# Edge attention in a graph network: the weighted sums of the values, in another number format and array shape

## What is computed

```python
qkv = x @ W_qkv.T + b_qkv
Q, K, V = jnp.split(qkv, [DK * HEADS, 2 * DK * HEADS], axis=-1)
...
scores = jnp.einsum('ehd,ehd->eh', Q[receivers], K[senders]) * scale
smax = jax.ops.segment_max(scores, receivers, num_segments=n_nodes)
ex = jnp.exp(scores - smax[receivers])
denom = jax.ops.segment_sum(ex, receivers, num_segments=n_nodes)
att = ex / denom[receivers]
out = jax.ops.segment_sum(att[:, :, None] * V[senders], receivers, num_segments=n_nodes)
```

## Time and profile before

| | |
|---|---|
| time before, median of 3 runs | 2308.41 us |
| lowest and highest run | 2305.57, 2312.28 us |
| the profiled execution: its own time | 2311.25 us |
| its span, first to last instruction | 2309.5 us |
| mean granted clock of TensorE, of full speed | 0.934 |
| TensorE busy (matmuls) | 1985.3 us, 86% |
| VectorE busy | 1403.4 us, 61% |
| ScalarE busy | 797.6 us, 35% |
| 1301 sums: 800 matmul records, 112.4 us | mean 287 ns |
| 1290 transposes: 800 records, 118.6 us | mean 280 ns |
| 1279 scores: 480 records, 115.1 us | mean 376 ns |
| 1346 minimum: 80, 116.8 us | mean 1460 ns |

### The profile page before, as it was taken

The page is one execution under the profiler, slowest core; times in us unless marked ns, Lnnn a source line. Parts: engine busy times, 40 slices in busy tenths (PEclk is TensorE's granted clock), DMA queues, the critical chain, the costliest instruction groups (busy, mean ns, idle before and its releaser), DMA issues. The chain is left out here.

```text
span 2309.5 us, 31827 instructions
## 1 busy us (share of the span) xinstructions
PE 1985.3 (86%) x10098; PEld 1147.6 (50%) x10099; DVE 1403.4 (61%) x3988; ACT 797.6 (35%) x1911; POOL 771.7 (33%) x849
## 2 busy tenths in 40 slices
PE   7987879889889888877769897699999884999997
PEld 4344343333333333333234453388888644777775
DVE  5885078988988988988753154288778643111111
ACT  2024134334343333343221230177777520222221
POOL 0000057777777777777700000011111000122221
PEclk9998989989989989989889898899999995999999
DMA  4012179999999999999930081535423143333351
GB/s 152 6 52 114 59 293 394 407 407 397 408 408 398 396 406 399 401 394 398 399 138 0 24 271 63 162 119 141 142 84 101 35 162 117 105 109 107 109 183 27
DMA packets 144378, 490.09 MB, mean 212 GB/s; under 512 B 16766, under 2 KB 17438, under 8 KB 144000
## 3 DMA queue, kind: packets, MB, share of 16 engines
q0 software_dynamic: 99952, 353.16, 40.5%
q1 hardware_dynamic: 44304, 135.43, 17.4%
HBM read 449.86 MB, written 38.67 MB: 212 GB/s over the span
## 5 line engine op out<-in xcount | busy, mean ns | idle before, releaser
L545 POOL DMA_INDIRECT m_ring<-in_table,m_rows_at x640 | 651.0, 1017 | 235.4 <-issue 130.8
L816 PE MATMUL m_acc<-m_ring,m_diag 64*64 64x512 f32 x2560 | 466.1, 699 | 131.7 <-ACT m_diag L716 131.1
L605 DVE CUSTOM_DVE_ANT_0 m_ring<-m_ring,m_coming,m_part 128x512 f32<-128x512 f32 x640 | 443.6, 749 | 47.6 <-DMA m_ring<-in_table,m_rows_at 37.2
L816 PEld LDWEIGHTS m_acc<-m_ring,m_diag 64*64 64x64 f32 x2560 | 152.1, 149 | 414.4 <-ACT m_diag L716 341.7
L716 ACT ACTIVATE m_diag<-m_eye,m_inner 128x64 f32<-128x64 f32 x640 | 222.3, 348 | 308.2 <-DVE m_inner L605 308.2
L1864 PEld LDWEIGHTS e_psU<-e_rowsT,x_w 128*128 128x128 f32 x1472 | 170.2, 194 | 14.1 <-issue 14.1
L1864 PE MATMUL e_psU<-e_rowsT,x_w 128*128 128x128 f32 x1472 | 170.7, 278 | 2.8 <-DMA x_w<-in_we 1.7
L1356 DVE TENSOR_TENSOR a_pT<-a_psT,a_pT 128x512 fp32r<-128x512 f32 (+1 forms) x240 | 140.1, 599 | 40.3 <-ACT a_pT L1391 37.0
L1873 PE MATMUL e_psY<-x_w,e_hT 128*128 128x512 f32 x368 | 161.7, 592 | 0.0
L1391 ACT ACTIVATE a_pT<-a_psT 128x512 fp32r<-128x512 f32 (+1 forms) x240 | 122.6, 528 | 97.5 <-PE a_psT L1290 97.5
L1290 PE MATMUL a_psT<-ident,a_prob 128*128 128x128 f32 x800 | 118.6, 280 | 28.4 <-ACT a_prob L1385 20.0
(11 more groups left out here) (326 smaller groups left out, 2705.6 us busy)
## 6 DMA issues: line engine op xcount, KB each, us to landing
x_w<-in_we SPq DMA_DIRECT2D x16, 2048.0 KB, 10.6
xnT<-edge_log_counts SPq DMA_DIRECT2D x40, 640.0 KB, 3.9
m_ring<-in_table,m_rows_at POOLq DMA_INDIRECT x640, 7.8
qk_parts<-p_parts SPq DMA_DIRECT2D x32, 320.0 KB, 4.2
a_k<-qk_parts SPq DMA_DIRECT2D x32, 320.0 KB, 9.2
edge_shares<-shareT SPq DMA_DIRECT2D x10, 640.0 KB, 3.0
m_share<-edge_shares SPq DMA_DIRECT2D x10, 640.0 KB, 7.4
edge_log_counts<-p_log_cnt SPq DMA_DIRECT2D x10, 640.0 KB, 6.2
```

The lines of the kernel that those rows point to most:

```text
L545: pool.indirect_dma_start(ring[:, slot, :], None, ins["table"], bass.IndirectOffsetOnAxis(rows_at[:, h, k:k + 1], 0)).then_inc(s_land[slot ...
L605: dve.tensor_tensor_reduce(ring[:, slot, 0:D], ring[:, slot, 0:D], coming[:, t % 2, :], part[:, b, k:k + 1], 0.0, ALU.mult, ALU.add, inner ...
L816: mm = pe.matmul(acc[to, i, :], diag[rows, h % 2 * TOPK + k, :], ring[rows, nth % RING, D:2 * D], start=h == 0 and k < 2, stop=h == HEADS ...
```

## The change

Probabilities and values are no longer split. `v` is float32, [P, NT, D]: VectorE adds the bias straight into it. The turned probabilities are copied once, in float32: piece 0 by ScalarE, pieces 1 and 2 by VectorE. The sums are made for four units at once (two node tiles of two heads): for each of ten sender tiles one float32 matmul for each head, stationary the 64 columns of that head, moving the 256 columns of its two node tiles; head 0 writes the partitions 0 to 63 of `psU`, head 1 64 to 127, so that each stands in one half of TensorE's columns. The result of four units is one [128, 256] tile, which two float32 transposes turn (`turn_back`); four `message` instructions follow. The matrix `fold` goes. The sums' pieces keep their places in TensorE's order, but for every fourth unit instead of every second.

```diff
@@ stage_projections
-        v_row = sb("v_row", [P, 2, D])
...
-                dve.tensor_tensor(v_row[:, t % 2, :], psV[:, t % 2, :], bv[:, :], ALU.add).then_inc(s["vout"], 1)
-                dve.drain()
-                rows = v_row[:, t % 2, :].rearrange("p (h d) -> p h d", h=HEADS)
-                dve.tensor_copy(v[:, t, :, 0, :], rows)
-                dve.drain()
-                dve.tensor_tensor(v[:, t, :, 1, :], rows, v[:, t, :, 0, :], ALU.subtract)
+                dve.tensor_tensor(v[:, t, :], psV[:, t % 2, :], bv[:, :], ALU.add).then_inc(s["vout"], 1)
@@ stage_edge_attention
-        prob, pT = sb("prob", [P, 2, NP]), sb("pT", [P, 2, NT, 2, P], F32R)
+        prob, pT = sb("prob", [P, 2, NP]), sb("pT", [P, NT, 2, 2, P])
...
                 if n:
-                    pe.wait_ge(s["rest"], 3 * n - 2 + piece)
+                    pe.wait_ge(s[f"copied{piece}"], n)
...
             def sums(g, piece):
-                m, t, h = unit(2 * g)
+                m = unit(4 * g)[0]
                 a, z = THIRDS[piece]
-                pe.wait_ge(s["rest"], 6 * g + 4 + piece)
+                pe.wait_ge(s[f"copied{piece}"], 4 * g + 4)
                 if piece == 0 and g:
                     pe.wait_ge(s["both"], g)
                 for x in range(a, z):
-                    for part in range(2):
-                        mm = pe.matmul(psU[:, 0:2 * P], v[:, x, 2 * m + h, :, :].rearrange("p a d -> p (a d)"),
-                                       pT[:, part, x, :, :].rearrange("p t n -> p (t n)"),
-                                       start=x + part == 0, stop=x + part == NT)
+                    for h in range(2):
+                        mm = pe.matmul(psU[64 * h:64 * h + 64, 0:2 * P], v[:, x, (2 * m + h) * 64:(2 * m + h + 1) * 64],
+                                       pT[:, x, h, :, :].rearrange("p t n -> p (t n)"), start=x == 0, stop=x == NT - 1)
...
-            def add_halves(g):
+            def turn_back(g):
                 pe.wait_ge(s["both"], g + 1)
                 if g:
-                    pe.wait_ge(s["msg"], 2 * g)
+                    pe.wait_ge(s["msg"], 4 * g)
                 for b in range(2):
-                    mm = pe.matmul(psM[:, 64 * b:64 * b + 64], both[:, b, :], fold[:, :], start=True, stop=True)
-                mm.then_inc(s["folded"], 1)
+                    mm = pe.transpose(psM[:, b * P:(b + 1) * P], both[:, b, :], c.ident[:, :])
+                mm.then_inc(s["back"], 1)
...
             for n in range(UNITS):
-                g = n // 2
-                if n % 2 == 0 and g:
+                g = n // 4
+                if n % 4 == 0 and g:
                     sums(g - 1, 1)
                 turn(n, 0)
-                if n % 2 == 0 and g:
+                if n % 4 == 0 and g:
                     sums(g - 1, 2)
                 turn(n, 1)
                 turn(n, 2)
                 if n + 2 < UNITS:
                     score(n + 2)
-                if n % 2:
+                if n % 4 == 3:
                     sums(g, 0)
-                elif g:
-                    add_halves(g - 1)
+                elif n % 4 == 0 and g:
+                    turn_back(g - 1)
@@ VectorE
-            def rest(n, piece):
+            def keep_turned(n, piece):
                 a, z = THIRDS[piece]
-                dve.wait_ge(s["high"], 3 * n + piece + 1)
-                dve.tensor_tensor(pT[:, 1, a:z, n % 2, :], psT[:, piece, 0:(z - a) * P].rearrange("p (a n) -> p a n", n=P),
-                                  pT[:, 0, a:z, n % 2, :], ALU.subtract).then_inc(s["rest"], 1)
+                m, tile, h = unit(n)
+                dve.wait_ge(s["turned"], 3 * n + piece + 1)
+                dve.tensor_copy(pT[:, a:z, h, tile % 2, :], psT[:, piece, 0:(z - a) * P].rearrange("p (a n) -> p a n", n=P))\
+                    .then_inc(s[f"copied{piece}"], 1)
...
             for n in range(UNITS):
-                rest(n, 0)
-                rest(n, 1)
+                keep_turned(n, 1)
+                keep_turned(n, 2)
                 if n + 2 < UNITS:
                     lowest(n + 2)
-                rest(n, 2)
-                if n % 2:
-                    shares(n // 2)
+                if n % 4 == 3:
+                    shares(n // 4)
@@ ScalarE
             for n in range(UNITS):
-                g = n // 2
-                high(n, 0)
-                high(n, 1)
-                if n % 2 == 0 and g:
+                g = n // 4
+                keep_turned(n)
+                if n % 4 == 0 and g:
                     keep_sums(g - 1)
                 if n + 1 < UNITS:
                     exponent(n + 1)
-                if n % 2 and g:
+                if n % 4 == 1 and g:
                     message(g - 1)
-                high(n, 2)
```

More of the change, by code:

```diff
@@ L1221, in stage_edge_attention @@
         q, k = sb("q", [P, 4, P], F32R), sb("k", [P, 2, 2, 2, NP], F32R)
-        prob, pT = sb("prob", [P, 2, NP]), sb("pT", [P, 2, NT, 2, P], F32R)
-        low, den, rden = sb("low", [P, 2]), sb("den", [P, 4]), sb("rden", [P, 4])
-        both, fold = sb("both", [P, 2, P]), sb("fold", [P, 64])
+        prob, pT = sb("prob", [P, 2, NP]), sb("pT", [P, NT, 2, 2, P])
+        low, den, rden = sb("low", [P, 2]), sb("den", [P, 8]), sb("rden", [P, 8])
+        both = sb("both", [P, 2, P])
         psS, psT, psU, psM = ps("psS", [P, 3 * D]), ps("psT", [P, 3, D]), ps("psU", [P, D]), ps("psM", [P, D])
-        names = ("score", "low", "exp", "turned", "high", "rest", "sums", "both", "folded", "msg", "rden", "pad", "fold", "ahead",
+        names = ("score", "low", "exp", "turned", "copied0", "copied1", "copied2", "sums", "both", "back", "msg", "rden", "pad", "ahead",
                  "q0", "q1", "q2", "q3", "k0", "k1", "log0", "log1", "log2", "log3")
@@ L1385, in exponent, with keep_turned @@
                 act.activation(prob[:, n % 2, 0:N], prob[:, n % 2, 0:N], ACT.Exp, bias=low[:, n % 2:n % 2 + 1], scale=-1.0,
-                               accum_out=den[:, n % 4:n % 4 + 1]).then_inc(s["exp"], 1)
-            def high(n, piece):
-                a, z = THIRDS[piece]
-                act.wait_ge(s["turned"], 3 * n + piece + 1)
-                act.activation(pT[:, 0, a:z, n % 2, :], psT[:, piece, 0:(z - a) * P].rearrange("p (a n) -> p a n", n=P),
-                               ACT.Copy).then_inc(s["high"], 1)
+                               accum_out=den[:, n % 8:n % 8 + 1]).then_inc(s["exp"], 1)
+            def keep_turned(n):
+                a, z = THIRDS[0]
+                m, tile, h = unit(n)
+                act.wait_ge(s["turned"], 3 * n + 1)
+                act.activation(pT[:, a:z, h, tile % 2, :], psT[:, 0, 0:(z - a) * P].rearrange("p (a n) -> p a n", n=P),
+                               ACT.Copy).then_inc(s["copied0"], 1)
             def keep_sums(g):
@@ L1396, in keep_sums @@
                 if g:
-                    act.wait_ge(s["folded"], g)
+                    act.wait_ge(s["back"], g)
                 act.activation(both[:, :, :], psU[:, 0:2 * P].rearrange("p (b n) -> p b n", b=2), ACT.Copy).then_inc(s["both"], 1)
             def message(g):
-                act.wait_ge(s["folded"], g + 1)
+                act.wait_ge(s["back"], g + 1)
                 act.wait_ge(s["rden"], g + 1)
-                for b in range(2):
-                    m, t, h = unit(2 * g + b)
-                    i = g % 2 * 2 + b
-                    act.activation(msg[:, m * NT + t, 64 * h:64 * h + 64], psM[:, 64 * b:64 * b + 64], ACT.Copy,
-                                   scale=rden[:, i:i + 1]).then_inc(s["msg"], 1)
+                for i in range(4):
+                    m, tile, h = unit(4 * g + i)
+                    at = g % 2 * 4 + i
+                    act.activation(msg[:, m * NT + tile, 64 * h:64 * h + 64], psM[:, i % 2 * P + 64 * h:i % 2 * P + 64 * h + 64],
+                                   ACT.Copy, scale=rden[:, at:at + 1]).then_inc(s["msg"], 1)
             exponent(0)
             for n in range(UNITS):
-                g = n // 2
-                high(n, 0)
-                high(n, 1)
-                if n % 2 == 0 and g:
+                g = n // 4
+                keep_turned(n)
+                if n % 4 == 0 and g:
                     keep_sums(g - 1)
@@ L1417, in _ @@
                     exponent(n + 1)
[L1418 removed]
+                if n % 4 == 1 and g:
                     message(g - 1)
[L1420 to L1422 removed]
+            keep_sums(UNITS // 4 - 1)
+            message(UNITS // 4 - 1)
 def stage_join(c, msg, weights, ahead):
```

22 lines of the change are left out of this document (9 added, 13 removed).

## The result

The changed kernel takes 2311.50 us, the median of 20 runs (2306.37 to 2318.07). The kernel before, beside it on the same chip, takes 2306.01 us (20 runs, 2300.79 to 2312.28). The ratio is 1.0019 with a 95% interval of 1.0010 to 1.0027. So the change costs about 4.4 us where 5.4 us of gain were forecast (4.4 is also the difference of the two means; the medians lie 5.5 apart). The time lies in the predicted range and within the 0.3% that was called no change, but the sign of the central forecast is wrong: the interval excludes any gain.

A forecast was written before the change was run, and what follows sets the result against it. TensorE was taken as nearly full before; afterwards score-minimum rounds plus lumped sums bound it. Exponentials 6.83 us less, the end 1.48 more: net gain 5.4 us, from 2308.41 to 2303.0 us; range 2295 to 2324.

The forecast's parts named there:

- the wake: Edge attention, from the minimum's end to the waiting score's start: 0.08 us, taken between 0.05 and 0.15, in 60 rounds.
- the change of shape: TensorE switching array shape between sums and scores or transposes: 0.09 us each, four a group, 0.36 us.
- the stage's end: Edge attention from the last exponential to the end: 9.38 us instead of 7.90, 1.48 more.
- The sums: TensorE's float32 sums for four units: column halves run together, 0.216 us a pair of passes, 4.32 us a group.
- The first rival: Weight loads of the sums not hidden: 0.10 us for each of 200 pairs, 20 us, 2323; chance 0.10.
- the second: Rival: the sums' column halves run one after the other, 4.3 us more in each of 20 groups, 2389; chance 0.05.
- The chain: Edge attention: one long step and three rounds of score and minimum (3.24 or 3.35 us), 16.87 us a group against 17.1.
- full drain: TensorE emptied at each change of shape: 0.16 us instead of 0.09, 5.6 us more over 80 changes, forecast 2309.
- The third rival: TensorE's clock falls in a group's 10 us without sums: 21 us for one round a group, 2324, all three 64; chance 0.05.
- the ends that the prediction named for them: Uncertainty in the edge attention: 60 wakes give -1.8 to +4.2 us, 80 changes of shape -7.2 to +5.6.
- TensorE's share in the stage: Sign in the edge attention: if TensorE's busy share stays at nine tenths, the forecast of score waits and rounds is wrong.
- a full TensorE: Rival: TensorE stays full and waits go, 14.3 us a group, 2252; said to be forbidden by one score buffer; chance 0.07.

The follow-up runs named there:

- the same-half kernel: The changed kernel with both heads' sums in the same column half, so their passes can't run side by side: 2393.79 us in one run.
- the first experiment: The changed kernel with the waits for queries, keys and new counts passed earlier, so score and minimum each wait for one thing: 2305.22 us, ratio 0.9988.
- second experiment: The changed kernel with all three thirds of a group's sums side by side, two changes of array shape a group instead of four: 2305.34 us, ratio 0.9988.
- the kernel in four places: The changed kernel with two buffers for turned probabilities, sums spread behind all four scores of the next group, and waits moved ahead: 2265.54 us, ratio 0.9805.

## Why the prediction was wrong

Two terms of its chain were too small, the wake, taken 60 times, and the change of shape, taken 80 times; together they used up the gain. That it became a loss comes mostly from the stage's end, where the forecast had put nothing for TensorE's lower clock. Point by point, by its own steps.

*The sums: right.* The passes start in pairs, and the pairs follow each other by 0.216 us. The first two, the first six and the first eight passes of a group, TensorE after the change, each from a narrower stretch:

```profile
1656.91 0.44 PE L1295 MATMUL a_psU<-a_pT,v 128*64 128x256 f32 x2
...
1656.91 0.87 PE L1295 MATMUL a_psU<-a_pT,v 128*64 128x256 f32 x6
...
1656.91 1.08 PE L1295 MATMUL a_psU<-a_pT,v 128*64 128x256 f32 x8
```

Two passes end 0.44 us after the first starts, two more cost 0.21 or 0.22. The first rival, loads that are not hidden, is out, and the same-half kernel shows what the second would have cost. The form that no row of before had, 128 rows by 64 columns, behaves as the quarters of the earlier trace rows suggested. The Trainium skill's page TensorE: Matmul & The Clock Gate, Part 3, The mechanism, lets a weight load pass a running matmul for another row group or into the background buffer. Here the row groups are the same and the loads (0.137 us each) cost the pairs nothing, so of the two only the second case can apply.

*The chain: right.* One long step and three rounds in each group, three waits for the minimum, VectorE's and ScalarE's relief off the path, nothing from the V products. The long part came out at 7.16 us where 7.04 were summed, the three rounds at 9.97 where 9.83 were: 0.26 us a group too little in all. Over 18 groups that makes 4.7 us; first to last exponential is 337.14 us where 331.83 were forecast, 5.3 more.

*The first failed step: the wake, 0.08 us.* It was taken between 0.05 and 0.15 and "nearer to the row at full clock". But the row of 0.05 is a sum that waits for one thing, and the only row in which this very score waited for the minimum said 0.15. I put that down to the half clock; the first experiment shows that it is the second wait. At full clock it is 0.15 too, and 0.06 without the second wait. Against this the round's other parts came out a little shorter (from the score's start to the minimum's 1.43 or 1.54 for 1.45 and 1.56), so that a round is 0.04 to 0.06 longer than forecast and not 0.07.

*The second failed step: the change of shape, 0.09 us.* What the 0.09 stood for came true: from the score's last pass (256 columns, fp32r) to the first sum is 0.21 us, where such a pass otherwise takes 0.12.

```profile
1656.70 0.28 PE L1273 MATMUL a_psS<-a_k,a_q 128*128 128x256 f32 x1
```

What it left out is that the first pass behind a change starts with its weight load and lasts 0.05 us longer: 0.430 instead of 0.379 for a sum, and four transposes behind a change take 0.66 where they took 0.60. So a change costs 0.14 to 0.15. In the timeline above, 32 passes take 3.60 us to the next transpose (16 pairs are 3.46, so 0.14), four transposes 0.59 to the next sum (0.44, so 0.15), eight passes 1.01 (0.86, so 0.15), six transposes 0.63 to the score (0.58 in the earlier trace rows, so 0.05), and from the score to the sums it is 1.33 for 1.26. Together 0.56 us a group against 0.36. Against this the transposes were priced too high, six at 0.66 where the earlier trace rows has 0.58 up to the score, so that the forecast's long part is 0.12 us too short and not 0.20. The rows had a hint of the 0.05: a pass that starts with its load lasts 0.64 us and one whose load came early 0.59. The prediction used that pair of durations for a rival and not for this term. The Trainium skill's page TensorEngine Tiling (Array Packing), Key Properties, has a change of tiling mode drain TensorE. The forecast named 0.16 us a change as its own price for a full drain and 2309 us as the result; with about 0.145 for a change, that reading was the nearer one.

*The third failed step: the stage's end, and the clock in it.* The tail was to take 9.38 us from the last exponential and took 10.78 (1823.51 to 1833.36 + 0.93). The rows of after:

```profile
1823.51 1.34 ACT L1376 ACTIVATE a_prob<-a_prob,a_low 128x1250 f32<-128x1250 f32 x1 [0.50 <-DVE a_low L1342]
...
1824.99 2.03 PE L1284 MATMUL a_psT<-ident,a_prob 128*128 128x128 f32 x10 [1.96 <-ACT a_prob L1376]
...
1826.95 5.45 PE L1295 MATMUL a_psU<-a_pT,v 128*64 128x256 f32 x40
...
1833.36 0.93 ACT L1398 ACTIVATE msg<-a_psM,a_rden 128x64 f32<-128x64 f32 x4 [0.53 <-PE a_psM L1305]
```

Ten transposes last 2.03 us instead of 1.31 and the sums 5.45 instead of 4.54 (second experiment). The clock is why; two stretches in this place:

```profile
1822.00:1825.40 3.40, 1.44 (x14) 1.20 (x13) 2.33 (x5) 2.44 (x6) 0.00 (x0) 1.00 0.00 0
1825.40:1828.80 3.40, 3.40 (x19) 2.31 (x19) 1.27 (x4) 0.60 (x1) 0.00 (x0) 0.50 0.00 0
```

TensorE was busy for 1.44 of 3.40 us and was then granted 0.50 for the next stretch, its lower level of 1.2 GHz. This is the third rival, in a place where I had not looked for it: in the rounds, at 1.00 from 1500 to 1780 us, it did not come true. The terms of the sum were sound: in the first two experiments, at full clock, the tail takes 9.25 us. But there the lower clock comes a little later, at the start of the join. The kernel of the first experiment, then the kernel before:

```profile
1818.81:1822.22 3.41, 1.09 (x9) 0.55 (x6) 0.32 (x1) 1.31 (x5) 0.00 (x0) 1.00 0.00 0
1822.22:1825.63 3.41, 3.41 (x10) 2.13 (x9) 0.37 (x1) 2.48 (x3) 0.00 (x0) 0.50 0.61 160
```

```profile
1832.20:1835.60 3.40, 2.16 (x11) 1.48 (x12) 0.69 (x1) 1.85 (x4) 0.00 (x0) 1.00 0.25 63
1835.60:1839.00 3.40, 3.40 (x13) 1.68 (x12) 0.69 (x1) 0.64 (x1) 0.00 (x0) 1.00 0.37 102
```

Of the ten traces, the kernel before and the one that only moves its waits have no such stretch between the last exponential and the end of the join. The other eight all have one, in the tail (both heads in one column half) or at the start of the join; the changed kernel alone has both, the second at 1835.70 to 1839.10. The join takes 56.8 us in the three traces without a low stretch in it, and 57.8 to 58.3 in the seven with one. So the 1.3 us there come with the longer tail, hardly by chance; the 1.4 us in the changed kernel's own tail are seen in the one trace that there is of it.

The account: between the 5.4 us less that were forecast and the 3.9 more of the profiled execution lie 9.3. Of these, 5.3 are between the first and the last exponential, from the rounds and changes of shape; 1.4 are in the tail and 1.3 in the join; 0.35 lie ahead of the first exponential, which comes 4.78 us after the first score instead of 4.43 (VectorE stands 0.44 us before its masking instruction, for no reason that the profile shows). The 0.9 that remain lie in other stages, and traces differ by that much where the code is the same: from the end of the join to the end they take 418.4 to 421.2 us. The line of the forecast was close to its own figure (0.40 each for faster and no change). Two terms of hundredths of a microsecond, taken 60 and 80 times, took the gain away; the clock and the rest made it a loss. Both errors lay inside the ends that the prediction named for them (+4.2 and +5.6), and for both I took a value below the one that was measured. The two ends together are 2312.8 us; the 2309 at which the prediction let its own case stop was less than their sum.

*A sign that was badly chosen.* "If TensorE's share in the stage stays at nine tenths, the chain is wrong": it is 248.64 of 280, 0.89 (0.92 before), and the chain is right. A pass of a pair is followed by the next pair after 0.216 us and is shown as lasting 0.379, so busy time closes over part of the gap at the end of each run of matmuls. The idle time before the scores, 33.3 us in 300, was the sign to name.

*What the prediction did not ask.* It costed the arrangement as given and stated that the transposes fit inside a round. The next question, what else would fit there, leads to the kernel in four places. That one score buffer forbids a full TensorE holds for this arrangement alone: the four-places kernel has TensorE full with the one buffer, at 14.78 us a group. The rounds are a bound only while they have less than 3.2 us of TensorE's work in them; spread evenly, every unit has 3.7.

## What to carry to other kernels

When an engine's work is cut, look at whether the rest still stands where that engine is the bound: with a latency loop between two engines (here score and minimum, 3.23 us), work moved into the loop's idle time costs little (a group fell from 17.17 to 15.42 us, though two changes of shape were added), and the same work in one lump is paid in full. Keep an instruction at the end of such a loop waiting for one thing; pass its other waits earlier, where time is idle. Price a term that occurs 60 or 80 times by the row that has the same wait and the same shapes, however odd its circumstances look, and read not only when the first instruction behind a change starts but also how long it takes. When a change makes the end of a stage emptier, look at the granted clock there and in the stage behind.

## What the runs showed of the hardware that was not expected

- A score that waits for the minimum and its queries starts 0.15 us after the minimum, one that waits for the minimum alone after 0.06; the round gets 0.06 shorter by it. A minimum that waits for the score and for new counts starts 0.11 us later than one that waits for the score alone.
- A change between 128 by 128 and 128 by 64 costs TensorE about 0.145 us: 0.09 until the first pass behind it starts, and 0.05 because that pass starts with its weight load.
- Two float32 matmuls over the same 128 rows, in the two column halves, run at the pace of one: 0.216 us for a pair of passes of 256 columns, weight loads hidden.
